# A three-layer graph attention network: probabilities rounded first and turned by the DMA crossbar, and every engine's order in a slot written anew

## The chip, the cores and the metric

The kernel runs on one core of a Trainium2 chip. A core has TensorE (PE) for matrix products, VectorE (DVE), ScalarE (ACT) and GpSimd (POOL) for elementwise work, and SyncE (SP), which here only issues DMAs. They run side by side, each through its own list in order, and wait for each other by semaphores. The metric is the device time of one execution in microseconds, the median of three runs.

## What is computed

`x` holds 128 graphs of 128 nodes with 256 features, `adj` a 128×128 adjacency matrix for each graph. The core of the reference:

```python
h = jnp.maximum(_layernorm(x), 0.0)
x = x + gnn(h, adj, ...)
# gnn, for each of 3 layers:
mask = adj.astype(jnp.float32) + jnp.eye(n) > 0
si = x @ attn_w[l, :d]
sj = x @ attn_w[l, d:]
scores = si[:, :, None] + sj[:, None, :] + attn_b[l]
scores = jnp.where(scores >= 0, scores, 0.2 * scores)
scores = jnp.where(mask, scores, -jnp.inf)
attn = jax.nn.softmax(scores, axis=-1)
agg = jnp.einsum('bij,bjd->bid', attn, x)
h = layernorm(x + agg, g1[l], beta1[l])
ff = jax.nn.gelu(h @ W1[l] + b1[l]) @ W2[l] + b2[l]     # 256 -> 1024 -> 256
x = layernorm(h + ff, g2[l], beta2[l])
```

All is float32. The kernel reaches that precision on TensorE by splitting each operand into a float16 high part and a float16 rest (names with `_hi` and `_lo`) and adding three products.

## The kernel before

**Items and slots.** Four graphs (T = 4) through one layer are an item; there are 32 groups × 3 layers = 96 items. Eight groups go through layer 0, then the same eight through layer 1, then layer 2. Each engine's program is a list of slots; slot s is cut into eight chunks c = 0 to 7, one for each 128 of the 1024 hidden columns. The program has an opening, four slots in the open, a loop of three rounds of 24 slots, and the rest in the open. Nothing but the order in which each engine's `slot` function is written, and the semaphores, sets what runs when.

**PE.** For chunk c of item s, `hidden` (L405) makes 128 hidden columns of four graphs: six matmuls of 512 columns into one of three PSUM buffers p_hid. Chunk c can begin once DVE has made `g_lo` of chunk c − 3. `feed` (L421) multiplies the chunk three places back by W2, twelve matmuls of 256 columns. At c == 3 PE spreads s_j of item s + 3 (`spread_sj`, four transposes by an identity, L455), at c == 4 it transposes the probabilities of item s + 2 (`transpose_probs`, L463), at c == 6 it multiplies them with X (`aggregate`, L477). Spreading waits until the second residual of item s − 1 has been read out of the shared PSUM bank (`res2_ready`).

**ACT.** For each chunk a gelu (L531) and a copy to float16 (L536). Between them it makes the high parts of X and h, the two layer norms' scaling (`norm_input` L548, at c == 7; `norm_attention` L555), the leaky scores and the exponentials (L560 to L567, at c == 5), and copies the transposed probabilities from PSUM to float16 (L571).

**DVE.** For each chunk `g_lo` (L645), the rest of gelu's result. Between them: the statistics of three layer norms (`statistics` L652, `aggregates` L657 to L660), masks (L673, L676), dot products for s_i and s_j (L690, L693), scores and row maxima (L709, L715), `low_probs` (L738), the attention residual (L728) and the feed residual (L749).

**POOL.** Inverse deviations (L897), the rests of X and h, the residual input h_res, the second norm and the layer's output. **SP** issues all loads and stores and two crossbar transposes a slot, of h's high and low part (L325).

A **start slot** is one in which a new group enters layer 0; input statistics, mask, `norm_input` and the loads are in these alone. The biases are folded into the first product by small float32 matmuls (`fold_bias`, L436), once for each layer, in the opening and in the slots named by `FOLD_AT`.

Of the kernel before, what the change touches and what calls it, by code (L numbers as in the profile page):

```python
# [35 lines left out]
P = 128  # L36
B, N, D = 128, 128, 256
L = 3
# [17 lines left out]
FOLD_AT = {3: 1, 5: 2}  # L56
# [68 lines left out]
def slots(eng, slot):  # L125

    for s in range(FIRST_LOOP_SLOT):
        slot(0, s)
    for r in range(LOOPS):
        for s in range(FIRST_LOOP_SLOT, FIRST_LOOP_SLOT + PER):  # L130
            slot(r, s)
    for s in range(FIRST_LOOP_SLOT, PER + 1):
        slot(LOOPS, s)


def gnn_kernel(nc, x, adj, attn_w, attn_b, W1, b1, W2, b2, g1, beta1, g2, beta2, out):
    with ExitStack() as ctx:
# [51 lines left out]
        pT_hi, pT_lo = sb("pT_hi", [P, TN], F16), sb("pT_lo", [P, TN], F16)  # L189
# [37 lines left out]

        def sj_bank(s):
            return p_pair[s % 2][:, 0:2, :].rearrange("p a (u n) -> p (a u) n", n=N)

        def pT_bank(s):
            return agg_banks(s)[:, 2:4, :].rearrange("p a (u n) -> p (a u) n", n=N)
# [21 lines left out]
        pT_psum = sem("pT_psum")  # L254
# [32 lines left out]
        act_pieces = dict(zip([(s, c) for s in range(4) for c in (0, 1)], pieces[4:]))  # L287
        dve_pieces = dict(zip([(s, c) for s in range(3) for c in (5, 6)] + [(3, 2), (3, 3)], pieces[4:]))
# [4 lines left out]
        def _(sp):  # L293
            def weights(l, n):
# [3 lines left out]
                if l >= 1 and n == 0:  # L298
                    sp.wait_ge(bias_psum, l)
# [8 lines left out]
            def load_x(g):  # L308
                sp.dma_start(x_in[g % 2][:], graphs(x, g)).then_inc(x_loaded[g % 2], 16)
# [9 lines left out]
            def turn_h(r, s):  # L319
                i = s % 2  # L320
                if later(r, s, 2):
                    sp.wait_ge(hid_psum, total(r, s - 2, C, C))
                for h, hT, made, turned in ((h_hi, hT_hi, h_hi_ready, hT_hi_ready), (h_lo, hT_lo, h_lo_ready, hT_lo_ready)):
                    sp.wait_ge(made, total(r, s, 1, 1))
                    sp.dma_start_transpose(hT[i][:].rearrange("p t k n -> p (t k) n"),  # L325
                                           h[:].rearrange("p t d -> p (t d)")).then_inc(turned, 16)

            def slot(r, s):
                if is_item(r, s + 4) and layer_of(s + 4) == 0 and group_of(r, s + 4) + 2 < G:
                    sp.wait_ge(x0_ready, group_total(r, s + 4, 4, 4))  # L330
                    load_x(group_of(r, s + 4) + 2)
                if is_item(r, s + 3) and layer_of(s + 3) == 0 and group_of(r, s + 3) + 2 < G:
                    sp.wait_ge(mask_steps, group_total(r, s + 3, 2, 2))
                    load_adj(group_of(r, s + 3) + 2)
                if (r, s) == (0, 1):
                    weights(2, 0)
                if is_item(r, s - 3) and layer_of(s - 3) == L - 1:
                    store(r, s - 3)
                if is_item(r, s + 1):
                    turn_h(r, s + 1)  # L340
                if (r, s) == (0, 1):
                    weights(2, 1)
# [10 lines left out]
            def next_x(g):  # L353
                sp.wait_ge(x0_ready, group_total(0, g - 2, 4, 4))
# [6 lines left out]
            def opening():  # L361
# [6 lines left out]
                columns(beta1_col, beta1, cols_dma)  # L368
                load_adj(1)
                weights(0, 0)  # L370
                next_x(2)
                next_adj(2)
                weights(0, 1)
                next_x(3)
# [5 lines left out]
                next_x(4)  # L380
                next_adj(4)
                attention_rows(slice(1, L))
# [3 lines left out]
                turn_h(0, 0)  # L386
                weights(1, 0)
                next_x(5)
# [15 lines left out]
        def _(pe):  # L404
# [31 lines left out]
            def fold_bias(l, bank):  # L436
# [3 lines left out]
                for c in range(C):  # L440
# [5 lines left out]
            def spread_sj(r, s):  # L446
# [4 lines left out]
                if isinstance(r, int) and r == 0 and s in FOLD_AT:  # L451
                    fold_bias(FOLD_AT[s], sj_bank(s))
# [5 lines left out]
            def transpose_probs(r, s):  # L458
                pe.wait_ge(probs_ready, total(r, s, 4, 4))
                if later(r, s, 3):  # L460
                    pe.wait_ge(res2_ready, total(r, s - 3, 2, 2))
                for t in range(T):
                    mm = pe.transpose(pT_bank(s)[:, t, :], probs[:, t, :], ident[:])  # L463
                mm.then_inc(pT_psum, 1)

            def aggregate(r, s):

                pe.wait_ge(pT_lo_ready, total(r, s, 1, 1))
                pe.wait_ge(X_lo_ready, total(r, s, 1, 1))
                if is_item(r, s + 1):  # L470
# [3 lines left out]
                for t in range(T):  # L474
                    nodes = slice(t * N, (t + 1) * N)
                    for n, (p, v) in enumerate(((pT_hi, X_hi), (pT_hi, X_lo), (pT_lo, X_hi))):
                        mm = pe.matmul(agg_banks(s)[:, t, :], p[:, nodes], v[:, t, :],  # L477
# [3 lines left out]
            def slot(r, s):  # L481
                for c in range(C):
# [5 lines left out]
                    if c == 4 and is_item(r, s + 2):  # L488
                        transpose_probs(r, s + 2)
# [5 lines left out]
                    if c == 3 and is_item(r, s + 3):  # L495
                        spread_sj(r, s + 3)
                    if c == 6 and is_item(r, s + 2):
                        aggregate(r, s + 2)
# [3 lines left out]
            def opening():  # L502
                pe.wait_ge(pool_steps, 4)
                spread_sj(0, 0)
                transpose_probs(0, 0)
                spread_sj(0, 1)
                aggregate(0, 0)
                fold_bias(0, fold_bank)
                transpose_probs(0, 1)
# [7 lines left out]
        def _(act):  # L517
# [26 lines left out]
            def norm_input(r, s):  # L544
# [3 lines left out]
                norm_apply(s, 0, x_in[s % 2], X[s % RING], ACT.Relu, x0_ready)  # L548
# [8 lines left out]
            def exponentials(r, s):  # L557
# [478 lines left out]
```

## Time and profile before

| | |
|---|---|
| median of three runs | 2315.44 us (2313.62 to 2316.35) |
| the profiled execution | 2317.27 us, its span 2315.5 us |
| busy over the span | PE 2247.7, PEld 1575.8, DVE 1793.1, ACT 1905.2, POOL 1872.8 us |
| mean granted clock of TensorE | 0.992 |
| share of DMA queue q1 (SP's) | 19.3% of 16 engines |

PE's busy time is near the span, but its matmuls are pipelined and their ends modelled; how long it takes over something is read from one start to the next. A busy time shows no reason for the span by itself: the stretches have to be looked at apart, and for each the wait that PE ends last.

### The profile page before, as it was taken

What the parts mean: (1) busy time and instruction counts of PE and PEld (TensorE: products, weight loads), DVE (VectorE), ACT (ScalarE), POOL (GpSimd) and SP (SyncE); (2) the same over time, 40 slices, a digit from 0 to 9 for tenths busy, and PEclk for the clock granted to TensorE, in tenths of its full rate; (3) what the DMA queues carried; (4) which work ended last, traced back from release to release, by engine and by line L of the source; (5) the groups of instructions that cost most, each with busy time, mean ns of one, the idle gap of its engine ahead of it and who ended that gap; (6) DMA issues with size and microseconds to landing.
All of it is one profiled execution on the core that took longest, in us unless ns stands there. A gap on an engine that the chain in (4) does not pass through costs nothing.

```text
span 2315.5 us, 46432 instructions
## 1 busy us (share of the span) xinstructions
PE 2247.7 (97%) x15840; PEld 1575.8 (68%) x15840; DVE 1793.1 (77%) x5887; ACT 1905.2 (82%) x3496; POOL 1872.8 (81%) x1642
## 2 busy tenths in 40 slices
PE   4899999999999999999999999999999999999998
PEld 3666777776667677777666767777766677777675
DVE  7677777778887777777888877777888877777765
ACT  6778888888888888888888888888888888888874
POOL 6467877888988787878898878787989887878786
PEclk9899999999999999999999999999999999999999
DMA  6321111124442111112443111111443211111133
GB/s 180 91 65 28 24 24 24 24 42 83 96 105 47 20 28 19 29 21 53 101 100 88 33 20 28 19 29 19 83 105 88 46 24 24 26 22 28 38 69 78
DMA packets 279273, 120.06 MB, mean 52 GB/s; under 512 B 209792, under 2 KB 277376, under 8 KB 279040
## 3 DMA queue, kind: packets, MB, share of 16 engines
q1 hardware_dynamic: 263200, 101.37, 19.3%
q0 software_dynamic: 15840, 15.73, 4.6%
q8 instruction: 128, 2.10, 0.4%
q14 instruction: 105, 0.86, 0.1%
HBM read 49.96 MB, written 16.78 MB: 29 GB/s over the span
## 4 chain that ended last, share of the span: by engine, by line
PE 75%; DVE 12%; ACT 8%; issue 3%; DMA 1%; POOL 1%; SPq 0%; DVEq 0%; POOLq 0%; ACTq 0%
PE p_hid L417 34%; PE p_pair L431 33%; PE p_pair L477 4%; DVE g_lo L645 2%; DVE bn L652 2%; PE p_pair L455 2%; ACT probs L566 2%; PE p_pair L463 1%; DVE res L728 1%; ACT p_hid L531 1%; ACT L531 1%; DVE res L749 1%; ACT L566 1%; ACT g_hi L536 1%; DVE adj_in L673 1%
## 5 line engine op out<-in xcount | busy, mean ns | idle before, releaser
L645 DVE TENSOR_TENSOR g_lo<-p_hid,g_hi 128x512 f16<-128x512 f32 x768 | 529.9, 690 | 475.7 <-ACT g_hi L536 469.2
L431 PE MATMUL p_pair<-w_hi,g_hi 128*128 128x256 f16 x3072 | 837.9, 273 | 0.0
L431 PE MATMUL p_pair<-w_lo,g_hi 128*128 128x256 f16 x3072 | 837.8, 273 | 0.0
L431 PE MATMUL p_pair<-w_hi,g_lo 128*128 128x256 f16 x3072 | 837.8, 273 | 0.0
L531 ACT ACTIVATE p_hid<-p_hid,b_eff 128x512 f32<-128x512 f32 x768 | 505.5, 658 | 310.0 <-PE p_hid L417 308.3
L897 POOL TENSOR_TENSOR rstd<-var_eps,minus_half 128x4 f32<-128x4 f32 x224 | 236.6, 1056 | 382.9 <-DVE minus_mean L660 382.8
L536 ACT ACTIVATE g_hi<-p_hid 128x512 f16<-128x512 f32 x768 | 459.3, 598 | 24.5
L417 PE MATMUL p_hid<-hT_hi,w_hi 128*128 128x512 f16 x1536 | 458.2, 380 | 6.5 <-DMA hT_hi<-h_hi 3.5
L417 PE MATMUL p_hid<-hT_lo,w_hi 128*128 128x512 f16 x1536 | 458.7, 380 | 0.9 <-DMA hT_lo<-h_lo 0.8
L417 PE MATMUL p_hid<-hT_hi,w_lo 128*128 128x512 f16 x1536 | 458.6, 380 | 0.0
L431 PEld LDWEIGHTS p_pair<-w_lo,g_hi 128*128 128x128 f16 x3072 | 300.8, 98 | 106.7 <-issue 0.3
L431 PEld LDWEIGHTS p_pair<-w_hi,g_hi 128*128 128x128 f16 x3072 | 300.9, 98 | 105.6 <-issue 0.3
L431 PEld LDWEIGHTS p_pair<-w_hi,g_lo 128*128 128x128 f16 x3072 | 300.8, 98 | 34.9
L417 PEld LDWEIGHTS p_hid<-hT_lo,w_hi 128*128 128x128 f16 x1536 | 150.3, 98 | 184.4 <-DMA hT_lo<-h_lo 3.5
L417 PEld LDWEIGHTS p_hid<-hT_hi,w_lo 128*128 128x128 f16 x1536 | 150.6, 98 | 182.2 <-issue 1.6
L652 DVE BATCH_NORM_STATS2 bn<-res 128x6 f32<-128x256 f32 x768 | 269.0, 414 | 3.3
L907 POOL TENSOR_TENSOR h_res<-norm,g_rows 128x1024 f32<-128x1024 f32 x96 | 240.6, 2506 | 0.0
L909 POOL TENSOR_TENSOR h_res<-h_res,res_rows 128x1024 f32<-128x1024 f32 x96 | 227.0, 2364 | 7.5
L915 POOL TENSOR_TENSOR h_lo<-norm,h_hi 128x1024 f16<-128x1024 f32 x96 | 219.7, 2289 | 1.5 <-ACT h_hi L586 1.4
L927 POOL TENSOR_SCALAR norm<-res,rstd,shift 128x256 f32<-128x256 f32 x380 | 211.3, 569 | 10.1 <-POOL shift L899 0.2
L541 ACT ACTIVATE norm<-res,shift,rstd 128x256 f32<-128x256 f32 x384 | 199.3, 592 | 18.8 <-POOL shift L899 18.5
L919 POOL TENSOR_TENSOR X_lo<-X,X_hi 128x1024 f16<-128x1024 f32 x96 | 205.4, 2140 | 0.0
(73 smaller groups left out, 3520.2 us busy)
## 6 DMA issues: line engine op xcount, KB each, us to landing
x_in<-in_x SPq DMA_DIRECT2D x32, 512.0 KB, 3.8
out<-w_f SPq DMA_DIRECT2D x31, 512.0 KB, 5.0
w_f<-in_x POOLq DMA_DIRECT2D x30, 512.0 KB, 6.1
adj_in<-in_adj SPq DMA_DIRECT2D x32, 256.0 KB, 4.4
w_f<-in_L_gnn_W SPq DMA_DIRECT2D x6, 1024.0 KB, 6.2
hT_hi<-h_hi SPq DMA_TRANSPOSE x96, 3.1
hT_lo<-h_lo SPq DMA_TRANSPOSE x96, 3.1
g_rows<-in_L_gnn_g SPq DMA_DIRECT2D x2, 384.0 KB, 6.6
```

The costliest lines, as they stand in the source:

```text
L417: mm = pe.matmul(p_hid[in_ring(s, c, PF_RING)][:], w[l][:, k, cols], h[i][:, :, k, :], start=(n == 0), stop=(n == 3 * KD - 1))
L431: mm = pe.matmul(ff_banks(s)[:, t, :], g[i][:, nodes], w[l][:, c, :], start=(c == 0 and t % 2 == 0 and n == 0), stop=(c == C - 1 and n == ...
L531: act.activation(p_hid[k][:], p_hid[k][:], ACT.Gelu, bias=b1_eff[:, l, c:c + 1], scale=1.0 / WSCALE).then_inc(gelu_ready, 1)
L536: act.activation(g_hi[i][:], p_hid[k][:], ACT.Copy).then_inc(g_hi_ready, 1)
L645: dve.tensor_tensor(g_lo[i][:], p_hid[k][:], g_hi[i][:], ALU.subtract).then_inc(g_lo_ready, 1)
L652: dve.bn_stats(bn[n][:, t, :], src[:, t, :]).then_inc(stat_steps[n], 1)
L897: pool.tensor_tensor(rstd[n][s % 2][:], var_eps[n][:], minus_half[:], ALU.pow).then_inc(rstd_ready[n], 1)
L907: pool.tensor_tensor(h_res[i][:], norm1[:], rows(g1_rows, l, T), ALU.mult).then_inc(h_res_steps, 1)
L909: pool.tensor_tensor(h_res[i][:], h_res[i][:], rows(res_rows, l, T), ALU.add).then_inc(h_res_steps, 1)
L915: pool.tensor_tensor(h_lo[:], norm1[:], h_hi[:], ALU.subtract).then_inc(h_lo_ready, 1)
L919: pool.tensor_tensor(X_lo[:], X[s % RING][:], X_hi[:], ALU.subtract).then_inc(X_lo_ready, 1)
L927: pool.tensor_scalar(norm2[:, t, :], res2[:, t, :], rstd[2][s % 2][:, t:t + 1], shift[2][s % 2][:, t:t + 1], ALU.mult, ALU.add).then_inc(n ...
```

## The change

The probabilities are no longer transposed in float32 by PE and then split. ACT rounds them to float16 (`p_hi`), DVE makes the rest (`p_lo`), and SP issues a crossbar transpose of each (`pT_hi`, `pT_lo`). `transpose_probs` is gone. The inputs of the third and fourth group are loaded straight into X[2] and X[3] and normalised there. Every engine's slot is written in another order: spreading at c == 4, feed residual at c == 1 (from 2), row scores at c == 3 (from 4), attention residual at c == 5 (from 7), dot products at c == 6 (from 5), `norm_input` for item s + 4 at c == 3 (for s + 5 at c == 7), exponentials at c == 6 behind the leaky scores at c == 5. On POOL the second norm of item s − 2 moves from the end of the slot before to the head of this one. Folds of layers 1 and 2 come a slot later, in two halves.

```diff
-FOLD_AT = {3: 1, 5: 2}
+FOLD_AT = {4: 1, 6: 2}
...
             def slot(r, s):
+                if is_item(r, s + 2):
+                    turn_probs_hi(r, s + 2)
+                    turn_probs_lo(r, s + 2)
...
+            def turn_probs_hi(r, s):
+                sp.wait_ge(p_hi_ready, total(r, s, 1, 1))
+                if later(r, s):
+                    sp.wait_ge(agg_ready, total(r, s - 1, 1, 1))
+                sp.dma_start_transpose(pT_hi[:], p_hi[:].rearrange("p t n -> p (t n)")).then_inc(pT_hi_ready, 16)
...
-            def transpose_probs(r, s):
-                pe.wait_ge(probs_ready, total(r, s, 4, 4))
-                if later(r, s, 3):
-                    pe.wait_ge(res2_ready, total(r, s - 3, 2, 2))
-                for t in range(T):
-                    mm = pe.transpose(pT_bank(s)[:, t, :], probs[:, t, :], ident[:])
-                mm.then_inc(pT_psum, 1)
...
             def aggregate(r, s):
 
-                pe.wait_ge(pT_lo_ready, total(r, s, 1, 1))
+                pe.wait_ge(pT_hi_ready, total(r, s, 16, 16))
+                pe.wait_ge(pT_lo_ready, total(r, s, 16, 16))
...
+            def high_probs(r, s):
+                act.wait_ge(probs_ready, total(r, s, 4, 4))
+                if later(r, s):
+                    act.wait_ge(pT_hi_ready, total(r, s - 1, 16, 16))
+                act.activation(p_hi[:], probs[:], ACT.Copy).then_inc(p_hi_ready, 1)
...
             def low_probs(r, s):
-                dve.wait_ge(pT_hi_ready, total(r, s, 1, 1))
-                dve.tensor_tensor(pT_lo[:].rearrange("p (t n) -> p t n", n=N), pT_bank(s),
-                                  pT_hi[:].rearrange("p (t n) -> p t n", n=N), ALU.subtract).then_inc(pT_lo_ready, 1)
+                dve.wait_ge(p_hi_ready, total(r, s, 1, 1))
+                if later(r, s):
+                    dve.wait_ge(pT_lo_ready, total(r, s - 1, 16, 16))
+                dve.tensor_tensor(p_lo[:], probs[:], p_hi[:], ALU.subtract).then_inc(p_lo_ready, 1)
...
+                    if c == 5 and is_item(r, s + 2):
+
+                        attention_residual(r, s + 2)
+                        attention_statistics(r, s + 2)
+                    if c == 6 and is_item(r, s + 2):
+                        aggregates(1, total(r, s + 2, 10, 8))
+                    if c == 6 and is_item(r, s + 4):
 
                         dot_products(r, s + 4, 0)
                         dot_products(r, s + 4, 1)
```

PE's list around the spreading of s_j (p_pair<-ident,s_j), in the loop. Before:

```order
L431 MATMUL p_pair<-w_hi,g_lo 128x256
L455 MATMUL p_pair<-ident,s_j 128x128 x4
L417 MATMUL p_hid<-hT_hi,w_hi 128x512 x2
L417 MATMUL p_hid<-hT_hi,w_lo 128x512 x2
L417 MATMUL p_hid<-hT_lo,w_hi 128x512 x2
L463 MATMUL p_pair<-ident,probs 128x128 x4
L431 MATMUL p_pair<-w_hi,g_hi 128x256
```

PE's list at the same place, now:

```order
L462 MATMUL p_pair<-w_hi,g_lo 128x256
L486 MATMUL p_pair<-ident,s_j 128x128 x4
L448 MATMUL p_hid<-hT_hi,w_hi 128x512 x2
L448 MATMUL p_hid<-hT_hi,w_lo 128x512 x2
L448 MATMUL p_hid<-hT_lo,w_hi 128x512 x2
L462 MATMUL p_pair<-w_hi,g_hi 128x256
L462 MATMUL p_pair<-w_lo,g_hi 128x256
```

The four transposes of the probabilities are gone, and the chunk behind spreading is now chunk 5, not chunk 4.

DVE's list from the attention residual (res<-p_pair,row_inv,X) over the slot's end to the feed residual (res<-p_pair,h_res), before:

```order
L645 TENSOR_TENSOR g_lo<-p_hid,g_hi 128x512 x2
L728 SCALAR_TENSOR_TENSOR res<-p_pair,row_inv,X 128x256 x4
L652 BN_STATS bn<-res 128x6 x4
L645 TENSOR_TENSOR g_lo<-p_hid,g_hi 128x512
L657 BN_AGGR mv<-bn 128x2 x4
L659 TENSOR_REDUCE var_eps<-mv 128x4
L660 TENSOR_REDUCE minus_mean<-mv 128x4
L645 TENSOR_TENSOR g_lo<-p_hid,g_hi 128x512 x2
L749 SCALAR_TENSOR_TENSOR res<-p_pair,h_res 128x512 x2
L645 TENSOR_TENSOR g_lo<-p_hid,g_hi 128x512
L652 BN_STATS bn<-res 128x6 x4
```

DVE's list from the feed residual to the attention residual, now:

```order
L787 SCALAR_TENSOR_TENSOR res<-p_pair,h_res 128x512 x2
L682 TENSOR_TENSOR g_lo<-p_hid,g_hi 128x512
L689 BN_STATS bn<-res 128x6 x4
L682 TENSOR_TENSOR g_lo<-p_hid,g_hi 128x512
L694 BN_AGGR mv<-bn 128x2 x4
L696 TENSOR_REDUCE var_eps<-mv 128x4
L697 TENSOR_REDUCE minus_mean<-mv 128x4
L746 SCALAR_TENSOR_TENSOR scores<-p_pair,s_i,mask 128x128 x4
L752 TENSOR_REDUCE row_top<-scores 128x4
L682 TENSOR_TENSOR g_lo<-p_hid,g_hi 128x512 x2
L765 SCALAR_TENSOR_TENSOR res<-p_pair,row_inv,X 128x256 x4
```

The attention residual stands two g_lo earlier in the slot; the statistics' aggregates and the dot products follow it before the last g_lo of the slot.

SP's list over a start slot in which a result is stored too (hT is the turned h, pT the turned probabilities), now:

```order
L338 DMA_TRANSPOSE pT_hi<-p_hi 128x4x128
L344 DMA_TRANSPOSE pT_lo<-p_lo 128x4x128
L315 DMA adj_in<-in_adj 128x4x128
L320 DMA out<-w_f 128x4x256
L326 DMA_TRANSPOSE hT_hi<-h_hi 128x8x128
L312 DMA x_in<-in_x 128x4x256
L331 DMA_TRANSPOSE hT_lo<-h_lo 128x8x128
```

Before, the three plain transfers stood ahead of the two transposes of h:

```order
L309 DMA x_in<-in_x 128x4x256
L312 DMA adj_in<-in_adj 128x4x128
L317 DMA out<-w_f 128x4x256
L325 DMA_TRANSPOSE hT_hi<-h_hi 128x8x128
L325 DMA_TRANSPOSE hT_lo<-h_lo 128x8x128
```

The load of x has moved between the two transposes of h, and two more transposes stand at the head.

## Rows read from the trace of the kernel before

**Rows 1.** Two stretches: busy us of each engine (x instructions), clock, DMA share, GB/s.
```profile
900.00:923.00 23.00, 23.00 (x166) 16.16 (x164) 17.29 (x57) 19.14 (x36) 18.40 (x17) 1.00 0.12 24
...
624.00:648.00 24.00, 23.34 (x166) 15.99 (x165) 20.73 (x69) 21.07 (x40) 21.44 (x20) 1.00 0.50 99
```

**Rows 2.** PE's timeline in an ordinary slot: start us, us, line, names, count.
```profile
1015.43 0.60 PE L455 MATMUL p_pair<-ident,s_j 128*128 128x128 f32 x4
1015.87 0.59 PE L417 MATMUL p_hid<-hT_hi,w_hi 128*128 128x512 f16 x2
...
1017.17 0.60 PE L463 MATMUL p_pair<-ident,probs 128*128 128x128 f32 x4
1017.60 0.27 PE L431 MATMUL p_pair<-w_hi,g_hi 128*128 128x256 f16 x1
...
1018.91 0.38 PE L417 MATMUL p_hid<-hT_hi,w_hi 128*128 128x512 f16 x1
```

**Rows 3.** PE's timeline, spreading of s_j alone [idle before <-what ended it].
```profile
203.65 0.60 PE L455 MATMUL p_pair<-ident,s_j 128*128 128x128 f32 x4
...
525.97 0.60 PE L455 MATMUL p_pair<-ident,s_j 128*128 128x128 f32 x4
...
693.09 0.62 PE L455 MATMUL p_pair<-ident,s_j 128*128 128x128 f32 x4 [0.82 <-DVE res L749]
...
992.41 0.60 PE L455 MATMUL p_pair<-ident,s_j 128*128 128x128 f32 x4
...
1107.53 0.60 PE L455 MATMUL p_pair<-ident,s_j 128*128 128x128 f32 x4
...
1251.87 0.62 PE L455 MATMUL p_pair<-ident,s_j 128*128 128x128 f32 x4 [1.05 <-DVE res L749]
...
1666.31 0.60 PE L455 MATMUL p_pair<-ident,s_j 128*128 128x128 f32 x4
...
1810.44 0.62 PE L455 MATMUL p_pair<-ident,s_j 128*128 128x128 f32 x4 [0.84 <-DVE res L749]
```

**Rows 4.** DVE's timeline in a start slot: mask, input statistics, feed residual.
```profile
682.42 1.35 DVE L673 CUSTOM_DVE_ANT_0 adj_in<-eye_i,adj_in 128x1024 uint16<-128x1024 uint16 x1
...
689.62 1.40 DVE L652 BATCH_NORM_STATS2 bn<-x_in 128x6 f32<-128x256 f32 x4
...
691.66 1.28 DVE L749 SCALAR_TENSOR_TENSOR res<-p_pair,h_res 128x512 f32<-128x512 f32 x2
```

**Rows 5.** Groups of instructions, whole run: the probabilities' low half.
```profile
L738 DVE TENSOR_TENSOR pT_lo<-p_pair,pT_hi 128x512 f16<-128x512 f32 x96 | 65.4, 681 | 1.3 <-ACT pT_hi L571 1.3
```

**Rows 6.** DMA issues (median us to landing), and one issue in SP's timeline.
```profile
hT_hi<-h_hi SPq DMA_TRANSPOSE x96, 3.1
...
beta_rows<-in_L_gnn_beta SPq DMA_DIRECT2D x1, 384.0 KB, 7.9
...
994.15 1.23 SPq L325 DMA_TRANSPOSE hT_hi<-h_hi  x1
```

**Rows 7.** DVE's timeline in an ordinary slot.
```profile
995.67 0.69 DVE L645 TENSOR_TENSOR g_lo<-p_hid,g_hi 128x512 f16<-128x512 f32 x1 [0.50 <-ACT g_hi L536]
...
999.94 0.47 DVE L690 CUSTOM_DVE_ANT_0 dots<-X,p_rows,attn_b_col 128x256 bf16<-128x256 f32 x1
...
1002.90 0.09 DVE L693 DVE_READ_ACCUMULATOR2_ANT s_j<- 128x1 f32 x1
...
1006.94 1.65 DVE L728 SCALAR_TENSOR_TENSOR res<-p_pair,row_inv,X 128x256 f32<-128x256 f32 x4
...
1011.22 0.68 DVE L645 TENSOR_TENSOR g_lo<-p_hid,g_hi 128x512 f16<-128x512 f32 x1
```

**Rows 8.** The opening: PE's timeline, and the stretch from 60 to 70 us.
```profile
42.57 1.01 PE L417 MATMUL p_hid<-hT_hi,w_hi 128*128 128x512 f16 x2 [3.53 <-DMA hT_hi<-h_hi]
...
66.06 6.99 PE L442 MATMUL p_pair<-beta_col,w_f 128*128 128x1 f32 x32 [8.92 <-DVE s_j L693]
...
60.00:70.00 10.00, 3.94 (x19) 3.94 (x19) 6.18 (x28) 3.72 (x7) 6.72 (x5) 0.50 0.79 220
```

More of the change, by code:

```diff
@@ L131, in slots @@
             slot(r, s)
-    for s in range(FIRST_LOOP_SLOT, PER + 1):
+    for s in range(FIRST_LOOP_SLOT, PER + 2):
         slot(LOOPS, s)
@@ L285, in gnn_kernel, with x_source @@
         pieces = [(l, n) for l in range(L) for n in range(4)]
-        act_pieces = dict(zip([(s, c) for s in range(4) for c in (0, 1)], pieces[4:]))
-        dve_pieces = dict(zip([(s, c) for s in range(3) for c in (5, 6)] + [(3, 2), (3, 3)], pieces[4:]))
+        act_pieces = dict(zip([(0, 6), (0, 7), (1, 0), (1, 3), (2, 0), (2, 3), (3, 0), (3, 3)], pieces[4:]))
+        dve_pieces = dict(zip([(0, 7), (1, 1), (1, 4), (2, 1), (2, 4), (2, 7), (3, 1), (3, 4)], pieces[4:]))
+        def x_source(r, s):
+            return X[s] if isinstance(r, int) and r == 0 and s in (2, 3) else x_in[s % 2]
         block = ctx.enter_context(nc.Block())
@@ new lines, in slot @@
+            def slot(r, s):
+                if is_item(r, s + 2):
+                    turn_probs_hi(r, s + 2)
+                    turn_probs_lo(r, s + 2)
+                if is_item(r, s + 3) and layer_of(s + 3) == 0 and group_of(r, s + 3) + 2 < G:
+                    sp.wait_ge(mask_steps, group_total(r, s + 3, 2, 2))
+                    load_adj(group_of(r, s + 3) + 2)
+                if is_item(r, s - 3) and layer_of(s - 3) == L - 1 and not (isinstance(r, int) and (r, s) == (LOOPS, PER + 1)):
+                    store(r, s - 3)
+                if is_item(r, s + 1):
+                    turn_h_hi(r, s + 1)
@@ L434, in feed, with fold_bias @@
                 mm.then_inc(ff_done, 1)
-            def fold_bias(l, bank):
+            def fold_bias(l, bank, half):
                 pe.wait_ge(w_dma[0], 16 * (l + 1))
                 pe.wait_ge(cols_dma, 2 * 16)
-                for c in range(C):
+                for c in range(C // 2 * half, C // 2 * (half + 1)):
                     for k in range(KD):
@@ L561, in exponentials @@
                 act.activation(leaky[:], scores[:], ACT.Prelu, alpha=SLOPE).then_inc(leaky_ready, 1)
+            def exponentials(r, s):
                 act.wait_ge(leaky_ready, total(r, s, 2, 2))
@@ L613, in opening @@
                 high_X(0, 0)
+                leaky_scores(0, 0)
+                exponentials(0, 0)
+                high_probs(0, 0)
                 norm_input(0, 1)
-                exponentials(0, 0)
-                copy_probs(0, 0)
+                norm_input(0, 2)
                 high_weights(0, 0)
                 high_weights(0, 1)
-                norm_input(0, 2)
+                norm_input(0, 3)
                 high_X(0, 1)
-                exponentials(0, 1)
                 norm_attention(0, 0)
                 high_h(0, 0)
+                leaky_scores(0, 1)
+                exponentials(0, 1)
+                high_probs(0, 1)
                 high_weights(0, 2)
                 high_weights(0, 3)
-                copy_probs(0, 1)
+                leaky_scores(0, 2)
                 exponentials(0, 2)
+                high_probs(0, 2)
             opening()
@@ L665, in input_statistics @@
                     dve.wait_ge(rstd_ready[0], group_total(r, s, 2, 0))
-                statistics(0, x_in[s % 2])
+                statistics(0, x_source(r, s))
             def make_mask(r, s):
@@ L838, in first_residual @@
                 attention_statistics(0, i)
+                dve.wait_ge(stat_steps[1], total(0, i, 10, 4))
+                aggregates(1, total(0, i, 10, 8))
             def opening():
@@ L976, in slot @@
                     h_residual(r, s + 1)
-                if is_item(r, s - 1):
-                    inverse_deviation(s - 1, 2, total(r, s - 1, 10, 10), total(r, s - 1, 2, 1))
-                    if not (isinstance(r, int) and (r, s) == (LOOPS, PER)):
-                        norm_feed(r, s - 1)
             def first_deviation(i, n):
```

224 lines of the change are left out of this document (114 added, 110 removed).

## The prediction

> **What bounds the kernel now.** I read the windows first, then the PE timeline, then the waits. From 900 to 923 us PE is busy for all of 23.00 us at granted clock 1.00, while ACT works 19.14, POOL 18.40 and DVE 17.29 us of it [rows 1]. So an ordinary slot is as long as PE's instruction list. Its parts come from starts in the PE timeline [rows 2]: spreading s_j takes 0.44 us (1015.43 to 1015.87), one chunk of the first matrix product (call it H) 1.30, the four probability transposes 0.43, one chunk of the second product (F) 1.31. Their records say 0.27 us apiece, but one starts every 0.11 us; the reader is to take starts, not durations, for a pipelined engine. A slot is 8 H + 8 F + one aggregation (12 matmuls like F's, 1.31) + spreading + transposes = 20.9 + 1.3 + 0.44 + 0.43 = 23.1; measured from spreading to spreading it is 1015.43 − 992.41 = 23.02 [rows 2, 3].
>
> Two stretches are longer. Three times in the run, six or seven slots in a row take about 24.05 us: 693.09 − 525.97 = 167.12 for 7 slots, 5.98 over 7 × 23.02; then 144.34 and 144.13 for 6 slots each, 6.22 and 6.01 over. Together 18.2 us. The bracket of the rows names what PE stands for there: spreading waits 0.8 to 1.05 us for DVE's feed residual (res, L749) [rows 3]. In such a start slot a new group of graphs begins, and DVE, ACT and POOL have 20.73, 21.07 and 21.44 us of work [rows 1], still under the period: it is an order that is late, not an engine that is full. DVE runs mask, attention residual, input statistics one behind the other and reaches the feed residual only at 691.66 [rows 4]. The other stretch is the opening, below.
>
> **The transposes leave PE.** 0.43 us in every slot. The first three of the 96 stand in the opening, where PE waits for others anyway, so 93 × 0.435 = 40.5 us. Below nothing this can't go, since the rest of PE's list is the same; it can be eaten by a new wait (rivals). The Trainium skill (VectorE: DVE Perf Modes, Rules for kernel authors) advises the opposite move, TensorE for a 128×128 transpose where PSUM will do and the crossbar otherwise. The trace agrees that TensorE is the quicker path for one block, not that it is the cheaper one here. The skill's page TensorE: Matmul & The Clock Gate, Part 4, gives about 275 ns for a transpose in a kernel; as an estimate by that page the move would be worth 93 × 4 × 0.275 = 102 us and the time 2182. The records' length agrees with it, their starts do not (0.11 us apart), and the starts decide.
>
> **What replaces them.** DVE's subtraction took 0.68 us with one operand in PSUM [rows 5] and now reads SBUF alone; ACT's copy to float16 does too. Bounds for each are 0.5 and 1.35 (the upper end is the mask instruction of [rows 4], the slowest DVE operation there that reads and writes SBUF); I take 0.68, the row of the same size and the same engine, so no change of load. At 1.35 the slacks below lose 0.7. New are two crossbar transposes per slot, half as large as those of h, which take SP 1.23 us to issue and land 3.1 us after it [rows 6]. I take 3.1 for landing; the bounds are half of that and 7.9, the slowest landing of all issues [rows 6].
>
> **Does the new order hold a 22.58 slot?** I lay one slot out from its start, with H 1.305, F 1.305 and starts as above. PE: H3 at 7.83, H4 10.44, then F1, spreading at 13.05, H5 13.49, H6 16.10, aggregation 17.40 to 18.71, F3, H7 20.02, next slot 22.58. A g_lo of DVE begins 2.82 us after its H (992.85 for H, that is spreading's 992.41 + 0.44; 995.67 for g_lo [rows 3, 7]) and H of chunk c needs g_lo of chunk c − 3.
> - The crossbar: probabilities are rounded behind ACT's H7 of the slot before, at about 2.4; the low half behind DVE's first g_lo at 5.4 (7.0 in a start slot). Issue 1.2 and landing 3.1 give 9.7 to 11.3; the aggregation wants it at 17.4. Cover: 6 us.
> - DVE's late half: its attention residual now stands behind g_lo 5, ahead of the aggregation it waits for, so DVE stands from about 17.0 to 18.87 with g_lo 6 and 7 queued behind it. From there 4.28 us to the end of the statistics' aggregates (1006.94 to 1011.22, the same sequence in the old order [rows 7]) gives 23.15, the dot products 3.0 (999.94 to 1002.90 and its read) 26.15 [rows 7], g_lo 7 ends at 26.84. PE wants it for H2 of the next slot at 22.58 + 5.22 = 27.80. Slack 0.96 us: the tightest place of the new order.
> - DVE's early half: feed residual waits for F7 of the item before, which ends at 8.0, and takes 1.28 [rows 4]: 9.3, against spreading at 13.05. In a start slot mask (1.75 with its second instruction), input statistics 1.4, aggregates 0.55, p_lo 0.7 and three g_lo lie between 26.8 and 32.3, so the feed residual ends at 10.9. Slack 2.1, where the old order had minus 0.8. So the 18.2 us should go; what is late next is g_lo 7, by the item above. Bounds: 0 to 18.2; I take all of it, since the slack is over twice the old shortfall.
> - ACT: norm_input moves from chunk 7, right before the next slot's first chunks, to chunk 3. Its 21.07 us of work fits 22.58; gelu 7, behind exponentials and a table load, ends at 24.5, before DVE asks at 26.1.
> - POOL: 21.44 of 22.58, cyclic order nearly as before. Its low half of h ends near 15 instead of near 20, so h lands earlier, although on SP a load of x now stands ahead of it.
>
> Sum for these: 40.5 + 18.2 = 58.7 us.
>
> **The opening.** From the first H at 42.57 [rows 8] to the spreading at 203.65 [rows 3] are 161.1 us; five slots and the four chunk pairs ahead of spreading are 5 × 23.02 + 10.44 = 125.5. Of the 35.6 too many, two folds of the bias (6.99 each [rows 8]) are 14.0 and stay: they are split in halves, the matmuls are the same. PE stands 8.92 us before the first of them, in slot 0, with W1's second layer not there; now that fold comes in slot 1, when the load has landed. The granted clock behind that wait is 0.50 in 60 to 70 us [rows 8], its lower level of 1.2 GHz, where PE had stood waiting and was busy 3.94 of 10 us; what runs there takes twice its time, some 5 us more over the fold, spreading and the first chunk behind it. Against it, DVE has the residual, an input and a dot product of the opening packed into slot 0 (8.6 us over a start slot), and probabilities of items 0 and 1 now cross the DMA queue behind loads at 3 to 5 us each, where TensorE and its copies took 2. I take 8.9 + 5 of clock − 2 = 12. Bounds: −8 (both latencies on the path, stall not gained) to 21.6 (all but the folds).
>
> The tail keeps its chain; it loses only what is counted above.
>
> **Sum.** The profiled execution's span is 2315.5 us, the device time beside it 2317.27, the median of the runs 2315.44, so the span stands for the median. 2315.5 − 40.5 − 18.2 − 12 = 2244.8; I say **2244**.
>
> **Rivals.**
> 1. The start slots stay late. For: DVE, ACT and POOL have only 1.1 to 1.9 us of room in 22.58, and a DMA share of 0.50 [rows 1] shows the transfers meeting there. Against: 2.1 us of slack at spreading. Time: 2244.8 + 18.2 = 2263. Chance 0.15.
> 2. The slack of 0.96 at g_lo 7 is not there, because DVE is held by in-order waiting on the aggregation. It decides from 1 us more on that chain; each 0.1 us beyond costs 9.3 us. With 0.45 beyond the slot is 23.0 again, the transposes' gain is gone, and 2244.8 + 42 = 2287 is left. For: four different waits meet on that chain. Against: every step has a row. Chance 0.11.
> 3. Slower than before: the crossbar's result comes later than 17.4 in each slot, as SP takes its waits in order (two transposes, adj, out, h high, x, h low in a start slot) and all transfers share one queue. It needs 6 us over the 9.7 to 11.3 above; at 7 us over, each slot is 1 us longer and 93 us are added: 2338. For: latencies of 7.9 in the opening. Against: 12% DMA share in ordinary slots. By the Trainium skill (VectorE: DVE Perf Modes, The three transpose paths) a 128×128 block takes the crossbar 1309 ns, so as an estimate four take 5.2 and the pair still lands near 14. Chance 0.05.
> 4. The opening gains all of its bound, 21.6: 2235. Chance 0.04.
>
> My forecast has 0.65, with its own range 2232 to 2256 from the opening's bounds. The range to hold 8 in 10 reaches over rival 1: 2230 to 2270. A change within 0.2% is what a measurement of this kernel can't tell from none; it needs a sum of losses of about 70 us and gets 0.02, slower 0.05, faster 0.93.
>
> **What would show it.** Spreading to spreading 22.58 in ordinary slots (transposes right), and the same between 525 and 693, with no wait on res (order right). PE waits named g_lo with 23 us slots would be rival 2; PE idle before the aggregation with a DMA as releaser, rival 3. The wait before the first fold gone and its clock at 1.00 would show the opening right. A slot above 23.02 anywhere in the middle makes the prediction wrong.

## The result, and the profile after

| | before | changed |
|---|---|---|
| median of the runs | 2314.65 us (4 runs) | 2275.43 us (4 runs, 2274.6 to 2275.7) |
| ratio, 95% interval | 1 | 0.983 (0.982 to 0.985) |
| span of the profiled execution | 2315.5 us | 2272.8 us |
| predicted | | 2244 us, range 2230 to 2270 |

Faster by 1.7%, and outside the range: the time is 31 us above the forecast. The first view is the windows of the changed kernel (busy us of PE, PEld, DVE, ACT, POOL with instructions, clock, DMA share, GB/s): an ordinary slot, then a start slot.

```profile
893.00:915.60 22.60, 22.60 (x163) 15.71 (x161) 17.75 (x57) 18.94 (x36) 18.78 (x17) 1.00 0.19 36
637.10:660.50 23.40, 22.93 (x162) 15.55 (x161) 22.45 (x71) 20.88 (x40) 21.85 (x21) 1.00 0.63 102
```

The ordinary slot answers to the first of [rows 1]: PE is still busy all the time, in 22.60 us instead of 23.00. In the start slot PE stands idle for a part of the time, and DVE has 22.45 us of work where [rows 1] had 20.73. The list of instructions hardly grew (71 against 69 in the stretch); some of them take longer, as the rows below show. Now the spreading of s_j in the PE timeline, which answers to [rows 3]:

```profile
204.75 0.60 PE L486 MATMUL p_pair<-ident,s_j 128*128 128x128 f32 x4
...
543.55 0.60 PE L486 MATMUL p_pair<-ident,s_j 128*128 128x128 f32 x4
566.95 0.60 PE L486 MATMUL p_pair<-ident,s_j 128*128 128x128 f32 x4
...
683.92 0.60 PE L486 MATMUL p_pair<-ident,s_j 128*128 128x128 f32 x4
706.74 0.60 PE L486 MATMUL p_pair<-ident,s_j 128*128 128x128 f32 x4
729.55 0.60 PE L486 MATMUL p_pair<-ident,s_j 128*128 128x128 f32 x4
752.14 0.60 PE L486 MATMUL p_pair<-ident,s_j 128*128 128x128 f32 x4
...
2185.69 0.60 PE L486 MATMUL p_pair<-ident,s_j 128*128 128x128 f32 x4
```

752.14 − 729.55 is 22.59 us, the ordinary slot (predicted 22.58). 566.95 − 543.55 is 23.40, and so it goes six times to 683.92; the two slots behind take 22.82. So each of the three groups has 6 × 0.81 + 2 × 0.23 = 5.3 us too many, 15.9 in all, where 18.2 had been. The bracket "<-DVE res" of [rows 3] is gone: the old cause went, another came.

The two profiled spans differ by 42.7 us. From item 8 to item 95 the time went from 2021.2 us to 1980.9: 87 × 0.435 = 37.8 us are the transposes, and 2.5 come from the start slots. The opening gave 1.5, since item 8 comes at 204.75 instead of 203.65, but one chunk pair, 2.6 us, later in its slot. The tail gave 0.9, which is what the last two items' transposes come to (2 × 0.435).

What DVE and POOL do in a start slot, DVE's timeline first (answers to [rows 4]), then POOL's, then PE's:

```profile
650.84 1.82 DVE L710 CUSTOM_DVE_ANT_0 adj_in<-eye_i,adj_in 128x1024 uint16<-128x1024 uint16 x1
652.70 1.38 DVE L713 TENSOR_SCALAR mask<-adj_in 128x512 bf16<-128x512 int32 x1
654.00 0.68 DVE L682 TENSOR_TENSOR g_lo<-p_hid,g_hi 128x512 f16<-128x512 f32 x1
654.60 1.15 DVE L777 TENSOR_TENSOR p_lo<-probs,p_hi 128x512 f16<-128x512 f32 x1
...
655.77 1.37 DVE L689 BATCH_NORM_STATS2 bn<-x_in 128x6 f32<-128x256 f32 x4
657.17 0.69 DVE L682 TENSOR_TENSOR g_lo<-p_hid,g_hi 128x512 f16<-128x512 f32 x1
```
```profile
650.85 1.27 POOL L981 TENSOR_TENSOR w_f<-norm,g_rows 128x512 f32<-128x512 f32 x1
652.20 1.60 POOL L988 TENSOR_TENSOR w_f<-w_f,beta_rows 128x512 f32<-128x512 f32 x1
653.75 1.46 POOL L981 TENSOR_TENSOR w_f<-norm,g_rows 128x512 f32<-128x512 f32 x1
```
```profile
654.74 0.61 PE L448 MATMUL p_hid<-hT_hi,w_hi 128*128 128x512 f16 x2
...
657.92 0.61 PE L448 MATMUL p_hid<-hT_hi,w_hi 128*128 128x512 f16 x2 [0.40 <-DVE g_lo L682]
```

The mask's two instructions take 1.82 and 1.38 us, and POOL's layer output starts with them to 0.01 us. Chunk 0's g_lo ends at 654.68 and H3 starts at 654.74, 0.22 late by PE's list. Then p_lo takes 1.15 and the input statistics 1.37, so that g_lo of chunk 1 comes only at 657.17 and H4 is 0.57 later again. The two make up the 0.81 but for 0.02. In the two slots behind, the mask still stands (1.81 and 1.37) and so does p_lo (1.15), but no input statistics: g_lo of chunk 1 follows p_lo almost at once, and only H3's 0.23 is left.

```profile
701.38 1.15 DVE L777 TENSOR_TENSOR p_lo<-probs,p_hi 128x512 f16<-128x512 f32 x1
...
702.54 0.65 DVE L682 TENSOR_TENSOR g_lo<-p_hid,g_hi 128x512 f16<-128x512 f32 x1
```

Behind item 8 all of PE's waits for g_lo are of this kind: there are 18, and none is for the g_lo 7 that rival 2 feared. Of DMAs only the turn of h's low half appears, twice, for 0.17 and 0.29 us.

### The profile page after: what moved, and what is told of

It reads as the page before. It is cut to its first block, busy times and chain, and to the rows that moved or that the text cites. A ratio compares the mean times of both kernels' runs of the same rounds, so it can differ in the third digit from the quotient of the medians.

```text
span 2272.8 us, 46153 instructions
## 1 busy us (share of the span) xinstructions
PE 2202.7 (97%) x15456; PEld 1520.7 (67%) x15456; DVE 1869.1 (82%) x5889; ACT 1887.6 (83%) x3496; POOL 1908.4 (84%) x1640
## 4 chain that ended last, share of the span: by engine, by line
PE 79%; DVE 17%; issue 3%; ACT 1%; DMA 1%; POOL 0%; DVEq 0%; SPq 0%
PE p_hid L448 36%; PE p_pair L462 35%; PE p_pair L500 5%; DVE g_lo L682 3%; DVE bn L689 3%; DVE res L765 2%; DVE adj_in L710 2%; DVE dots L727 2%; PE p_pair L486 2%; DVE dots L730 1%; DVE p_lo L777 1%; DVE mv L694 0%; PE p_pair L473 0%; DMA pT_hi<-p_hi 0%; DMA adj_in<-in_adj 0%
## 5 line engine op out<-in xcount | busy, mean ns | idle before, releaser
L682 DVE TENSOR_TENSOR g_lo<-p_hid,g_hi 128x512 f16<-128x512 f32 x768 | 518.0, 683 | 44.0 <-ACT g_hi L561 36.1
L937 POOL TENSOR_TENSOR rstd<-var_eps,minus_half 128x4 f32<-128x4 f32 x224 | 230.5, 1029 | 266.1 <-DVE minus_mean L697 266.1
L765 DVE SCALAR_TENSOR_TENSOR res<-p_pair,row_inv,X 128x256 f32<-128x256 f32 x384 | 159.3, 477 | 157.1 <-PE p_pair L500 157.1
L959 POOL TENSOR_TENSOR X_lo<-X,X_hi 128x1024 f16<-128x1024 f32 x96 | 219.3, 2284 | 13.1 <-ACT X_hi L610 13.1
```

The source lines that it names most:

```text
L682: dve.tensor_tensor(g_lo[i][:], p_hid[k][:], g_hi[i][:], ALU.subtract).then_inc(g_lo_ready, 1)
L937: pool.tensor_tensor(rstd[n][s % 2][:], var_eps[n][:], minus_half[:], ALU.pow).then_inc(rstd_ready[n], 1)
L959: pool.tensor_tensor(X_lo[:], X[s % RING][:], X_hi[:], ALU.subtract).then_inc(X_lo_ready, 1)
```

## The experiments

Medians, and ratios to the kernel before with their 95% intervals, fastest first. The kernel before was measured anew beside each group of experiments and gave 2313.7 to 2316.9 us. So the ratio is each kernel's own comparison, and a difference of 3 us between the medians of two experiments says little by itself.

| kernel | median, us | ratio |
|---|---|---|
| both repairs and slot 0 rearranged (4) | 2253.37 | 0.9722 (0.9708 to 0.9735) |
| both repairs (4) | 2254.11 | 0.9727 (0.9714 to 0.9741) |
| mask first (1) | 2256.83 | 0.9754 (0.9740 to 0.9769) |
| POOL's pieces short, a part of the result left out (2) | 2260.58 | 0.9760 (0.9746 to 0.9773) |
| opening alone (3) | 2271.59 | 0.9815 (0.9800 to 0.9829) |
| changed kernel | 2275.43 | 0.9831 (0.9816 to 0.9846) |
| crossbar twice (7) | 2277.87 | 0.9838 (0.9823 to 0.9853) |
| order only (5) | 2301.68 | 0.9935 (0.9922 to 0.9949) |
| old order with p_lo early (6) | 2313.08 | 0.9986 (0.9977 to 0.9996) |
| crossbar in the old order (5) | 2439.89 | 1.0539 (1.0522 to 1.0557) |

**1. The mask moved ahead of the dot products.**
```
-  c == 6: dot_products(s+4)          c == 7: make_mask(s+4)
+  c == 6: make_mask(s+4)             c == 7: dot_products(s+4)
```


> The changed kernel with two pieces of DVE's slot exchanged: the mask (two instructions) stands at c == 6 behind the statistics' aggregates, the dot products at c == 7 behind g_lo 7. Theory A (the mask and p_lo meet POOL's tensor-tensor products and both slow down: 1.82 + 1.38 us for the mask against 0.68 + 0.43 alone, 1.15 against 0.68 for p_lo; that makes g_lo 0 and g_lo 1 late): at the new place POOL runs only its 128x4 operations, so the mask takes some 1.1 us, start slots fall from 23.39 to 22.6 to 22.8 us and the time from 2275 to about 2260. Theory B (DVE's list in a start slot is too long by its number of instructions, whatever stands beside it; or the mask is slow because of the DMA that fills adj): mask durations stay at 1.8 + 1.4, start slots stay at 23.2 to 23.4, time 2270 to 2276.

Measured: 2256.83 us (2255.86 to 2260.19). All slots between item 8 and item 95 are 22.59. The mask's groups (ns: min/median/max), in the changed kernel and then in this one:

```profile
L710 DVE CUSTOM_DVE_ANT_0 adj_in<-eye_i,adj_in x29: 681/1817/1825, 8.1 to 1815.2; 128x1024 uint16<-128x1024 uint16 x29
L713 DVE TENSOR_SCALAR mask<-adj_in x29: 426/1378/1386, 8.8 to 1817.1; 128x512 bf16<-128x512 int32 x29
```
```profile
L710 DVE CUSTOM_DVE_ANT_0 adj_in<-eye_i,adj_in x29: 680/681/704, 8.4 to 1793.1; 128x1024 uint16<-128x1024 uint16 x29
L713 DVE TENSOR_SCALAR mask<-adj_in x29: 426/427/455, 9.1 to 1793.8; 128x512 bf16<-128x512 int32 x29
```

The same work takes 1.11 us in its place beside POOL's small rstd and shift, and 3.20 beside its layer output. The whole 15.9 us come back, and 2.9 more in the opening (item 8 at 201.88). Of itself this does not tell contention from place, since both were changed. It does tell the mask from p_lo: in the start slots, but for the first of a group, p_lo now takes 1.61 to 1.80 us where the changed kernel had 1.15, and they are on time all the same.

```profile
646.63 1.79 DVE L777 TENSOR_TENSOR p_lo<-probs,p_hi 128x512 f16<-128x512 f32 x1
```

**2. POOL's pieces short, the mask left where it is.** A first try made them short only where the group number is a register:
```
+  cut = slice(0, 8) if l == L - 1 and not isinstance(r, int) else slice(0, D)
```


> The changed kernel in which POOL makes only 8 of 256 columns of the last layer's output in the loop, so this part of the result is left out; nothing moves on DVE. Theory A (DVE's mask is slowed by POOL's tensor-tensor work beside it): in start slots whose POOL writes the last layer's output the mask takes some 0.7 + 0.43 us and p_lo 0.7 again, and these slots fall to about 22.6; time about 2262. Theory B (the mask is slow by itself at this place, by DMA or by its own data): the mask keeps 1.8 + 1.4 us, start slots stay at 23.4, time 2275.

Measured: 2276.2 us, one run. Its trace still has POOL's pieces at full width: every slot is written out with an integer, so the condition is never met and this is the changed kernel again. It says nothing on the theories, but it is a second profile of the same program, which is of use in experiment 4. The second try goes by the slot; it leaves out 248 of the 256 columns of the layer output in the slots named:
```
+  cut = slice(0, 8 if s % PER in (18, 19, 20, 21, 22, 23, 0, 1) else D)
   pool.tensor_tensor(dst[:, pair, cut], norm2[:, pair, cut], rows(g2_rows, l)[:, :, cut], ALU.mult)
```


> The changed kernel; GpSimd's layer_output works on 8 of the 256 columns of each graph for the items whose output falls into a start slot (the rest of these columns is left out of the result), so its tensor-tensor pieces of 1.27 and 1.60 us are all but gone while VectorE's mask stays in its new place. Theory A (the mask is slow because GpSimd's pieces run beside it): the mask's two instructions fall from 1.82 and 1.38 us to about 0.7 and 0.45, H3 and H4 come in time, start slots go from 23.39 to at most 22.8 us, and the time from 2275 to about 2260. Theory B (the place alone costs, whatever runs beside it): 23.39 and 2275 stay.

Measured: 2260.58 us (2260.34 to 2261.97). DVE's order is that of the changed kernel, and of the 24 late slots 18 are at 22.59 (in each group the first is 24.33 and the last 22.80). So the durations decided, not the place itself: theory A. The timeline of DVE, and of POOL, in one such slot:

```profile
645.36 0.69 DVE L710 CUSTOM_DVE_ANT_0 adj_in<-eye_i,adj_in 128x1024 uint16<-128x1024 uint16 x1
646.08 0.43 DVE L713 TENSOR_SCALAR mask<-adj_in 128x512 bf16<-128x512 int32 x1
647.02 0.68 DVE L777 TENSOR_TENSOR p_lo<-probs,p_hi 128x512 f16<-128x512 f32 x1
```
```profile
645.36 0.77 POOL L982 TENSOR_TENSOR w_f<-norm,g_rows 128x16 f32<-128x16 f32 x1
646.21 0.38 POOL L989 TENSOR_TENSOR w_f<-w_f,beta_rows 128x16 f32<-128x16 f32 x1
```

The slot of 24.33 us shows the same thing the other way round (DVE, then POOL): POOL's next job, X_lo, has come forward and meets p_lo.

```profile
555.66 3.46 DVE L777 TENSOR_TENSOR p_lo<-probs,p_hi 128x512 f16<-128x512 f32 x1
```
```profile
555.94 2.63 POOL L959 TENSOR_TENSOR X_lo<-X,X_hi 128x1024 f16<-128x1024 f32 x1
```

p_lo (0.68 alone) ends at 559.12, some 0.55 after POOL's X_lo at 558.57: nearly its own length after it, as if it ran only then. X_lo took 2.63 us; its median in the changed kernel is 2.14.

**3. The opening.**
```
   ACT:  - norm_input(0, 3) ahead of high_X(0, 1)
         + norm_input(0, 3) behind high_probs(0, 1)
   POOL: + low_X(0, 1), low_h(0, 0) ahead of first_deviation(3, 0)
```


> The changed kernel with the opening alone in another order: ACT scales the fourth input behind the rounding of item 1's probabilities, not ahead of item 0's attention norm, and POOL makes the low parts of X and h ahead of the fourth input's deviation. Theory A (the opening's gain went to one wait: ACT stands 12.1 us for the fourth input's shift with item 0's norm, which was ready 6 us earlier, queued behind): the first H moves from 49.05 to 43 to 45 us, the time falls by 4 to 6 us, to about 2270. Theory B (the crossbar's latency for items 0 and 1 and the loads ahead of it in the queue set the start): the first H stays within 1.5 us of 49 and the time at 2275.

Measured: 2271.59 us (2269.61 to 2272.89); item 8 at 200.19 instead of 204.75. In the changed kernel ACT stands for input 3 with item 0's attention norm queued behind, and the first H comes late (ACT's timeline, then PE's):

```profile
39.76 2.07 ACT L566 ACTIVATE X<-X,shift,rstd 128x256 f32<-128x256 f32 x4 [12.11 <-POOL shift L939]
```
```profile
49.05 1.01 PE L448 MATMUL p_hid<-hT_hi,w_hi 128*128 128x512 f16 x2 [5.24 <-DMA hT_hi<-h_hi]
...
67.85 1.03 PE L448 MATMUL p_hid<-hT_hi,w_hi 128*128 128x512 f16 x2 [6.62 <-DVE g_lo L682]
...
94.08 1.95 PE L473 MATMUL p_pair<-beta_col,w_f 128*128 128x1 f32 x16 [1.00 <-DVE res L787]
```

First H at 49.05 where [rows 8] had 42.57; with the repair it is 45.38, close to what theory A said. So ACT's order accounts for 3.7 of these 6.5 us; the other 2.8 were not traced. The second row is new too: in slot 0 PE waits 6.62 us for DVE's chunk 1, which stands behind a residual, two input statistics, p_lo and a wait for POOL. The third answers to the fold of [rows 8]: its wait is 1.00 instead of 8.92.

**4. Both repairs, and slot 0 rearranged as well.**
```
   slot 0 of DVE: first_residual(1) behind chunk 0; first_input(4), low_probs, row_sums
+  behind chunk 1; input_statistics(5) behind chunk 2; its aggregates behind chunk 3
```


> The changed kernel with both repairs: the mask ahead of the dot products (2256.8 alone) and the opening's normalisation of input 3 behind the probabilities of item 1 (item 8 came 4.6 us earlier with it alone). Theory A (the two places have nothing to do with each other): 2256.8 minus 4 to 5 = 2252 to 2253. Theory B (the opening's gain is taken back by the first start slots): 2257.

> As the kernel with both repairs, and in slot 0 VectorE does input 4's statistics, the probabilities' rounding rest and the statistics of input 5 behind later chunks of the hidden layer, so that chunk 1 waits behind the attention residual of item 1 alone. Theory A (the 6.6 us that TensorE waits in slot 0 come from VectorE's work in chunk 0): most of it goes, 3 to 6 us, 2247 to 2249. Theory B (GpSimd then takes the deviation of input 4 later, with that of item 1 queued behind it, and the wait comes back at item 1's H): 2252, no change.

Measured: 2254.11 (2249.61 to 2255.51) and 2253.37 (2248.14 to 2253.4). Reckoned from item 0's spreading, item 8 comes 188.5 us later with the mask first alone, 187.5 with both, 185.8 with slot 0 too; and the profiled spans are 2254.0, 2253.7 and 2251.6. So in these profiles 1 is left, beside the other repair, of the 4 to 5 us that the opening was worth alone. The first median lies between the two theories: 2.7 below the mask alone; the ratios say, each against its own kernel before, some 6. How much is left stays open. Of slot 0's wait of 6.6 us about 1.7 came through, which is nearer to theory B's time; the rest was given back before item 8 (the slot to item 4 is 36.05 us long with slot 0 rearranged, 30.75 without), and what took it was not traced.

One part of the small gain can be read: the slot to item 7 takes 24.31 us with both repairs and 22.64 with the mask alone. The windows of that slot's start, both repairs first:

```profile
154.57:160.00 5.43, 5.43 (x26) 3.25 (x27) 4.71 (x8) 1.87 (x4) 5.35 (x3) 0.69 0.63 91
```
```profile
156.65:162.00 5.35, 5.35 (x37) 3.70 (x38) 4.62 (x8) 2.60 (x6) 5.27 (x3) 1.00 0.59 87
```

PE is busy in both, but the granted clock is 0.69 in one and 1.00 in the other, just behind the second fold of matmuls one column wide. The repair is not the cause: the changed kernel has the same slot at 22.86 us, and the first try of experiment 2, which is the same program, has it at 24.52. The start of that slot in these two, the changed kernel first:

```profile
159.30:164.70 5.40, 5.40 (x38) 3.74 (x39) 4.14 (x8) 2.65 (x6) 4.25 (x3) 1.00 0.42 104
```
```profile
159.58:165.00 5.42, 5.41 (x25) 3.07 (x26) 4.23 (x8) 1.87 (x4) 2.28 (x3) 0.69 0.18 36
```

So 1.7 us of such a difference between two profiles can come and go from one execution to the next. Both versions beat the two kernels given; between them these runs can't choose.

**5. The two halves of the change apart.** The order without the crossbar, and the crossbar without the order:
```
   new order:  PE transposes probs in chunk 4, ACT and DVE split them from PSUM there
   old order:  ACT p_hi behind chunk 6, DVE p_lo in chunk 4, two turns on SP; no transposes on PE
```


> The new order with the old way: probabilities are transposed by TensorE into PSUM in chunk 4 and split by ScalarE and VectorE there; nothing goes through the crossbar. Theory A (the two halves add up: the transposes cost 0.435 us a slot in any order, and the new order costs nothing else): ordinary slots 22.59 + 0.435 = 23.02 us, start slots about 23.3 because p_lo no longer stands ahead of chunk 1's g_lo, in all 2275 + 38 - 10 = 2303. Theory B (the order only works with the crossbar; VectorE's split in chunk 4 makes g_lo 5 late): ordinary slots 23.2 or more and 2320 or more.

> The kernel before with only the probabilities' way changed: rounded first, turned by the crossbar, no transposes on PE; every engine's order otherwise as before. Theory A (all the gain of ordinary slots is the removed PE work, and the new order's share is in the start slots alone): ordinary slots 22.59 us, start slots stay at the old order's 24.05, so 2315 - 70 x 0.435 = about 2284, give or take 4 for the opening. Theory B (the new order is needed for ordinary slots too, since the crossbar's result comes too late for the aggregation in the old one): ordinary slots above 22.8, time above 2295.

Measured: 2301.68 us (2299.57 to 2303.21) for the order alone, with slots of 23.02 and start slots of 23.28; 2439.89 (2437.67 to 2441.28) for the crossbar alone, with slots of 24.00, start slots of 24.48 and four slots of some 30. The order alone is worth 15 us; the crossbar is worth some 26 more on top of it (24 by the ratios), and costs 126 without it. The start slots of the order-only kernel bear out the reading above. Their mask is as slow (1.80 and 1.38), but no p_lo stands ahead of chunk 1's g_lo, and they are 0.26 us too long instead of 0.81. In the crossbar-only kernel p_lo stands in chunk 4 and PE waits for the aggregation (DVE, then SP, then PE):

```profile
1020.12 1.74 DVE L757 TENSOR_TENSOR p_lo<-probs,p_hi 128x512 f16<-128x512 f32 x1
```
```profile
1021.89 1.19 SPq L340 DMA_TRANSPOSE pT_lo<-p_lo  x1
```
```profile
1024.38 0.27 PE L494 MATMUL p_pair<-X_hi,pT_hi 128*128 128x256 f16 x1 [0.71 <-issue]
```

From 1021.89 the 2.4 us to landing, its median in this run, end at 1024.3, and the aggregation starts at 1024.38. In the first of the slots of some 30 us the wait at the same place is 4.40 us; why was not traced.

**6. The old order, p_lo early.** The chunk of that subtraction alone, and its turn on SP:
```
-  c == 4: low_probs(s + 2)      SP: p_hi, h_hi, p_lo, h_lo
+  c == 0: low_probs(s + 2)      SP: p_hi, p_lo, h_hi, h_lo
```


> The old order with the crossbar, but with VectorE's rounding rest p_lo moved from chunk 4 to chunk 0 and its turn put right behind that of p_hi on SyncE's queue. Theory A (the crossbar in the old order lost its gain only because p_lo was made in chunk 4, two chunks ahead of the aggregation): PE no longer waits 0.7 us there, ordinary slots go from 24.00 to 22.6 to 22.8 and the time from 2440 to 2290 to 2310. Theory B (the old order as a whole holds the scores, maxima and residual too late for a slot of 22.59 us, whatever is done with p_lo): ordinary slots 23.0 or more, at least 2330.

Measured: 2313.08 us (2309.8 to 2313.98), slots of 22.71 where the crossbar-only kernel had 24.00, start slots of 24.40. One subtraction in the wrong chunk had cost 1.3 us of every slot. The first theory's ordinary slots came true, its total missed by the start slots, which stay those of the old order and even grow.

**7. The crossbar twice.**
```
+  sp.dma_start_transpose(spare[:], p_hi[:]...)     # ahead of each turn of p_hi
   sp.dma_start_transpose(pT_hi[:], p_hi[:]...)
```
Only p_hi is turned twice, since a second spare tile had no room in SBUF; the expectation speaks of both halves.

> The changed kernel with every turn of a rounded probability tensor issued twice on SyncE's queue, first into a spare tile and then into its own, so that each half's result comes one issue (1.2 us) and part of a transfer later. Theory A (the crossbar's result has some 9 us to spare: pT_lo is issued at 1016.15, lands 2.4 us later and is read at 1027.5): ordinary slots stay at 22.59 us and the time at 2275. Theory B (its result is nearly the last thing that the aggregation waits for, so cover is thin): every slot grows by 1 us or more, 2350 or more.

Measured: 2277.87 us (2277.05 to 2278.64), ordinary slots 22.59: theory A. The few us stand in the opening (item 8 at 207.72, 3.0 later, with a slot to item 7 of 24.53 like that of experiment 4) and two start slots (23.89, 24.39). So 96 more turns on the queue, and a high half that comes 1.24 us later in its slot, cost the ordinary slots nothing. The low half, the later of the two, kept its place, so the run does not measure how far that one could slip; by the changed kernel's trace it is issued at 1016.15, has landed 2.4 us later, and is read about 9 us after that. Median landings (us) with the double turn:

```profile
spare<-p_hi SPq DMA_TRANSPOSE x96, 2.4
pT_hi<-p_hi SPq DMA_TRANSPOSE x96, 2.5
pT_lo<-p_lo SPq DMA_TRANSPOSE x96, 2.4
```

## Why the prediction was wrong

- **Transposes, 40.5 us: right.** Slots of 22.59 against 22.58, and a start every 0.11 us rather than 0.27 was the right way to count. The order-only run confirms it: 23.02 with them, 22.59 without. At the 275 ns each that the prediction quotes from the Trainium skill (TensorE: Matmul & The Clock Gate, Part 4) the slots would have been 21.9; the records are 0.27 us long here too, but the starts decide.
- **"So the 18.2 us should go … Slack 2.1": the failed step.** 2.3 were gained (18.2 − 15.9). The slack was worked out for spreading, where it holds (no wait on res is left). It was not worked out for H3 and H4, which need g_lo 0 and g_lo 1: the first now stands behind the mask, the second behind mask, p_lo and input statistics. By the prediction's own numbers (32.3, less 0.55 for the aggregates and 22.58 for the slot) g_lo 1 ended near 9.15 against H4 at 10.44, 1.3 us of slack. Two mis-sized durations, 1.9 us together, ate that: "mask (1.75 with its second instruction)" is 3.2 us, since it was read beside the neighbours of its old place [rows 4], and "I take 0.68" for p_lo is 1.15. The 1.35 us of [rows 4] had itself been a stretched duration: the same instruction took 0.68 in 7 of its 28 places in the kernel before. The working did hold the upper bound of 1.35 for p_lo, and named rival 1 with 2263; but neither was put into the slack at H4, nor was the mask given a bound. Rival 1, start slots late, is what happened, though not by its reasons: POOL and DVE had room for their work, since with the mask elsewhere all of it fits into 22.59 us, and the DMAs did not slow the mask, since cutting POOL's pieces alone cured it.
- **The cause, shown:** with the mask elsewhere the start slots are 22.59, and with POOL's pieces cut short 18 of the 24 are. The mask's two instructions and p_lo, all on SBUF, stretch when POOL works on full tiles beside them, while g_lo, which reads one operand from PSUM, does not (684 ns in the median over 768, at most 693). To read SBUF alone is not enough for it: the row maxima took 686 to 687 ns beside the same POOL work, and a statistics instruction never more than 430. p_lo had been of the g_lo kind until the change brought its operand from PSUM into SBUF: 681 ns [rows 5], now

```profile
L777 DVE TENSOR_TENSOR p_lo<-probs,p_hi x96: 679/1219/1800, 21.6 to 2199.4; 128x512 f16<-128x512 f32 x96
```

  The Trainium skill (SBUF — State Buffer, Who interferes with whom) has the rule: a VectorE instruction with two SBUF inputs contends with a GpSimd instruction that reads SBUF, one in a two-port mode (which a tensor-scalar can enter) contends with GpSimd too, the one blocks the other fully, and issue order decides which. On the blocking the traces agree: p_lo ended 0.55 us after X_lo, the mask's first instruction 0.54 after POOL's first piece. On the order no run here shows it: the profile has p_lo begin 0.28 us ahead of the X_lo that it ended behind. The prediction should have weighed the rule.
- **The opening, 12 us: wrong, the second failed step.** 1.5 came. The stall of 8.92 ahead of the fold went, as predicted, but the first H came 6.5 us later and slot 0 got a wait of 6.62; both are instructions queued behind others (ACT's behind input 3, DVE's g_lo behind the pieces of chunk 0), where the text had put 2 us for DVE's packing and the crossbar. Experiment 3 shows the first for 3.7 of its 6.5 us. The granted clock in 60 to 70 us rose from 0.50 to 0.80, but PE was busy only 3.38 us of it:

```profile
60.00:70.00 10.00, 3.38 (x18) 1.64 (x16) 8.62 (x42) 3.75 (x9) 4.85 (x5) 0.80 0.72 187
```
- **Rival 2 (g_lo 7) and rival 3 (crossbar late): did not occur.** The slack of 0.96 held, and a high half 1.24 us later cost no ordinary slot anything. Rival 3 named the right danger for the wrong order: in the old one the crossbar makes each slot 24.00 us.
- **The sum:** 2244.8 + 15.9 for the start slots + 10.5 for the opening = 2271.2 of the span's 2272.8. The rest is that outside the opening 37.8 + 0.9 of the 40.5 us of transposes came; the other 1.8, for items 3 to 6, fall into the opening, whose whole gain was 1.5.

## What to carry to other kernels

When an instruction moves, its duration doesn't move with it: look up what VectorE and GpSimd run side by side in the new place, above all for those that take both operands from SBUF, and after replacing a PSUM operand by one in SBUF. A duration read from a profile already holds what ran beside it; take the shortest of the same instruction for what it costs alone. Work out the slack for every consumer of the chunk in front of which something is put, not only for the one that was late before. Taking a load off the bounding engine pays only as far as the replacement arrives in time: the same crossbar was worth 26 us in one order, 3 us with p_lo early, and −126 us in the old one.

## What the runs showed of the hardware

- The mask instruction of 0.68 us took up to 1.83, its second of 0.43 up to 1.39, p_lo of 0.68 up to 3.46, beside GpSimd's work on full tiles. GpSimd's own pieces of 1.27 us grew too: to 1.60 beside the mask, and to 1.73 beside p_lo where that had begun earlier (mask first).
- A crossbar turn of four 128×128 blocks landed 2.4 us after issue, against 3.1 predicted for it from the turn of twice the size.
- The granted clock was 0.69 over 5.4 us in which PE was busy throughout, right behind matmuls one column wide, so for a part of them it was below its upper level of 2.4 GHz; in the 5 us behind it was 1.00. Of two profiles of the same program one had this dip and the other 1.00 there; the slot was 1.7 us longer with it.
